# A selective-scan decoder layer: for three of sixteen state indices GpSimd makes u·B in SBUF and ScalarE writes the decay into PSUM

## What is computed

```
xz = x @ W_in.T;  x_ssm, z = split(xz)
x_ssm = silu(causal_conv(x_ssm, 4 taps) + conv_b)
proj = x_ssm @ W_x.T;  B, C = proj[:, 0:16], proj[:, 16:32]
dt = softplus(proj[:, -1:] * W_dt + b_dt);  A = -exp(A_log)
for t in tokens:                       # for every channel d and state n
    h = exp(dt[t] * A) * h + (x_ssm[t] * dt[t]) * B[t]
    y[t] = sum over n of h * C[t]
out = ((y + x_ssm * D) * silu(z)) @ W_out.T
```

## Time and profile before

| | |
|---|---|
| median of 3 runs | 1765.63 us (1763.73 to 1768.42) |
| the profiled execution | 1757.35 us |
| its span in the profile | 1755.6 us |
| granted clock of TensorE, mean | 0.915 of full speed |
| VectorE, TensorE busy | 1421.3 us (81%), 1418.8 us (81%) |
| ScalarE, GpSimd busy | 1151.1 us (66%), 899.1 us (51%) |
| start of the second stage | 1000.2 us |

### The profile page before, as it was taken

One profiled execution on the slowest core, in us unless ns is written; L12 is line 12 of the kernel. 1 busy time (PEld: TensorE's weight loads), 2 busy tenths in 40 slices (PEclk: granted clock), 3 DMA queues, 4 the chain that ended last, 5 costly groups with the idle time before them and its releaser, 6 DMA issues. The chain is left out here.

```text
span 1755.6 us, 23166 instructions
## 1 busy us (share of the span) xinstructions
PE 1418.8 (81%) x7740; PEld 987.4 (56%) x7740; DVE 1421.3 (81%) x2646; ACT 1151.1 (66%) x2516; POOL 899.1 (51%) x659
## 2 busy tenths in 40 slices
PE   7677777877787778778869799888998899888980
PEld 5566665666566656656656445472656355544570
DVE  5999999999999999999999533874667554964578
ACT  5877888788877887788775253377335843476471
POOL 1778777778788878887786000016200630055015
PEclk9799889898989899998989899999999999999895
DMA  7110111011102110121020211000200010000000
GB/s 234 59 55 1 67 67 55 13 67 67 55 13 67 67 62 6 67 67 61 1 85 13 79 34 52 1 1 1 76 1 1 1 45 4 1 1 1 25 1 24
DMA packets 38185, 70.07 MB, mean 40 GB/s; under 512 B 3569, under 2 KB 31826, under 8 KB 33842
## 3 DMA queue, kind: packets, MB, share of 16 engines
q1 hardware_dynamic: 38066, 68.60, 11.5%
HBM read 59.94 MB, written 8.65 MB: 39 GB/s over the span
## 5 line engine op out<-in xcount | busy, mean ns | idle before, releaser
L900 POOL TENSOR_TENSOR state_c<-state,c_area 128x1024 f32<-128x1024 f32 x256 | 600.9, 2357 | 169.4 <-DVE state L970 150.2
L970 DVE TENSOR_TENSOR_SCAN state<-decay,ps 128x512 f32<-128x512 f32 x512 | 620.6, 1212 | 0.0
L686 ACT ACTIVATE decay<-step_area,negA 128x255 f32<-128x255 f32 x1024 | 433.0, 497 | 0.5 <-DVE step_area L1049 0.5
L1577 POOL TENSOR_TENSOR big<-big,g_sb 128x1024 f32<-128x1024 f32 x29 | 78.8, 2718 | 578.9 <-ACT big L1471 577.6
L945 DVE TENSOR_TENSOR ps<-step_area,ps 128x512 f32<-128x512 f32 x512 | 349.9, 684 | 8.3 <-PE ps L368 6.9
L384 PE MATMUL ps<-ident_sb,state_c 128*128 128x128 f32 x2048 | 292.7, 290 | 13.4 <-POOL state_c L900 12.4
L384 PEld LDWEIGHTS ps<-ident_sb,state_c 128*128 128x128 f32 x2048 | 252.4, 150 | 39.8 <-POOL state_c L900 22.4
L368 PE MATMUL ps<-parts,sel_bc_sb 96*128 96x256 bf16 x256 | 74.5, 292 | 104.3 <-DVE ps L961 81.3
L1395 PE MATMUL ps<-w_sb,weights 128*128 128x512 f32 x256 | 129.3, 644 | 0.0
L1430 PE MATMUL ps<-w_sb,hT 128*128 128x256 f32 x512 | 118.9, 386 | 2.5 <-ACT hT L1546 1.9
L1531 ACT ACTIVATE big<-ps 128x1024 f32<-128x1024 f32 x32 | 32.8, 1024 | 121.1 <-PE ps L1395 121.1
(11 more groups left out here) (211 smaller groups left out, 2513.1 us busy)
## 6 DMA issues: line engine op xcount, KB each, us to landing
c_area<-c_scratch SPq DMA_DIRECT2D x32, 1024.0 KB, 6.6
weights<-in_xT SPq DMA_DIRECT2D x16, 256.0 KB, 3.2
res<-in_x SPq DMA_DIRECT2D x16, 256.0 KB, 2.9
x_scratch<-res SPq DMA_DIRECT2D x16, 256.0 KB, 7.9
weights<-x_scratch SPq DMA_DIRECT2D x4, 1024.0 KB, 7.7
xa<-x_scratch SPq DMA_DIRECT2D x4, 1024.0 KB, 5.5
out_x<-acc SPq DMA_DIRECT2D x4, 1024.0 KB, 4.2
w_sb<-in_w SPq DMA_DIRECT2D x2, 1024.0 KB, 12.9
```

Of the source, the lines that this page charges most:

```text
L686: nc.scalar.activation(decay[:, n % RING, j, 1:], dt_sb[:, i[1] % 2, j, 1:], ACT.Exp, scale=negA[:, j * NS + n:j * NS + n + 1]).then_inc(s ...
L900: nc.gpsimd.tensor_tensor(state_c[:, n % RING, :, :], state[:, n % RING, :, :], c_bc[:, q, n, :].unsqueeze(1).to_broadcast([P, CT, TC]), A ...
L970: nc.vector.tensor_tensor_scan(state[:, n % RING, pair, :].rearrange("p j n -> p (j n)"), decay[:, n % RING, pair, :].rearrange("p j n -> ...
L1577: nc.gpsimd.tensor_tensor(tile, tile, g2_sb[:, :], ALU.mult).then_inc(s_gm, 1)
```

## The change

For the states n = 3, 6 and 9 (`OFF`) of every chunk VectorE no longer makes u·B and no longer adds the carry. GpSimd makes the product of 128 x 1024 in SBUF (`product_b`, a ring of two tiles `ub`) from rows of B that a DMA has spread over the partitions (`b_bc`), and adds the carried state into the first column of each tile. ScalarE writes the decays of these states into PSUM (`psum_decay`): the first half into the bank of `b_ps` that is not needed for a row of B, the second into a bank of the three `bu_ps`, with a copy of zeros into the first columns. It does so one state later than before: after its own work for state n+1. The scan of these states reads the decay from PSUM and u·B from SBUF. TensorE issues no `b_row` for them, and `b_row` of state n+2 waits for the first scan of state n.

GpSimd makes the product of state 6 at its place 2, that of state 9 at place 5, and that of state 3 of the next chunk at place 15 (for the first chunk ahead of its first state). SyncE stores 32 rows of B and C instead of 16, and issues one more spreading DMA per chunk, of three rows. To make room in SBUF, w1 and w2 are loaded at the start of the second stage.

```diff
+        OFF, APART = (3, 6, 9), 3
...
+        def bu_free(i, n, h):
+            p = USERS.index((n, h))
+            return scanned(i if p >= 3 else shift(i, -1), *USERS[p - 3])
...
             def load_c(k):
                 q = k[1] % 2
                 sp.wait_ge(s_projc, at(k, 2, 1))
-                sp.dma_start(c_dram[bass.ds(at(k, NS), NS), :], proj[NS:BC, q, :]).then_inc(s_cst, 16)
+                sp.dma_start(bc_dram[bass.ds(at(k, BC), BC), :], proj[0:BC, q, :]).then_inc(s_cst, 16)
                 count = at(k, 16, 16)
                 sp.wait_ge(s_cst, count)
+                if not is_first(k):
+                    sp.wait_ge(s_ub, at(k, 2 * NO))
+                rows = bc_dram[bass.ds(at(k, BC, OFF[0]), APART * NO), :].rearrange("(a s) n -> a s n", s=APART)
+                sp.dma_start(b_bc[:, :, :], rows[:, 0, :].partition_broadcast(P)).then_inc(s_bb, 16)
                 sp.wait_ge(s_y, count)
...
             def b_row(i, n):
+                if n in OFF:
+                    return
                 if n == 0:
                     pe.wait_ge(s_split, at(i, 2, 2))
-                pe.wait_ge(s_bu, at(i, 4 * NS, 4 * n + 4))
+                if n - 2 in OFF:
+                    pe.wait_ge(s_scan, scanned(i, n - 2, 0))
...
             def step(i, n):
-                for j in range(CT):
-                    if j == 0:
-                        if n == 0:
-                            act.wait_ge(s_dt, at(i, 1, 1))
-                        act.wait_ge(s_scan, at(i, 2 * NS, 2 * n + 2))
-                        if n >= RING or not is_first(i):
-                            nc.scalar.activation(carry[:, (n - RING) % NS, :], state[:, n % RING, :, TC - 1],
-                                                 ACT.Copy).then_inc(s_carry, 1)
-                    nc.scalar.activation(decay[:, n % RING, j, 1:], dt_sb[:, i[1] % 2, j, 1:], ACT.Exp,
-                                         scale=negA[:, j * NS + n:j * NS + n + 1]).then_inc(s_decay, 1)
+                act.wait_ge(s_scan, at(i, 2 * NS, 2 * n + 2))
+                if n == 0:
+                    act.wait_ge(s_dt, at(i, 1, 1))
+                if n >= RING or not is_first(i):
+                    nc.scalar.activation(carry[:, (n - RING) % NS, :], state[:, n % RING, :, TC - 1],
+                                         ACT.Copy).then_inc(s_carry, 1)
+                if n in KEPT:
+                    for j in range(CT):
+                        nc.scalar.activation(decay_tile(i, n)[:, j, 1:], dt_sb[:, i[1] % 2, j, 1:], ACT.Exp,
+                                             scale=negA[:, j * NS + n:j * NS + n + 1]).then_inc(s_decay, 1)
+                if n - 1 in OFF:
+                    psum_decay(i, n - 1)
+
+            def psum_decay(i, n):
+
+                for h in range(2):
+                    if h == 0:
+                        act.wait_ge(s_bu, at(i, 4 * NK, 8 + 4 * rank(n - 2) + 3))
+                    else:
+                        act.wait_ge(s_scan, bu_free(i, n, 1))
+                    bank = (b_ps[n % 2] if h == 0 else bu_bank(i, n, 1))[:, :].rearrange("p (j n) -> p j n", j=2)
+                    nc.scalar.activation(bank[:, :, 0], zeros[:, :], ACT.Copy)
+                    for e in range(2):
+                        j = 2 * h + e
+                        nc.scalar.activation(bank[:, e, 1:], dt_sb[:, i[1] % 2, j, 1:], ACT.Exp,
+                                             scale=negA[:, j * NS + n:j * NS + n + 1]).then_inc(s_decay, 1)
...
+            def product_b(i, n):
+
+                c, later = OFF.index(n), i[1] % CPB
+                if c == 0:
+                    pool.wait_ge(s_u, at(i, 1, 1))
+                    pool.wait_ge(s_bb, at(i, 16, 16))
+                if c >= 2:
+                    pool.wait_ge(s_scan, scanned(i, OFF[c - 2], 1))
+                elif not is_first(i):
+                    pool.wait_ge(s_scan, scanned(shift(i, -1), OFF[c - 2], 1))
+                tile = ub_tile(i, n)
+                nc.gpsimd.tensor_tensor(tile, u_sb[:, i[1] % 2, :, :], b_bc[:, c, :].unsqueeze(1).to_broadcast([P, CT, TC]),
+                                        ALU.mult).then_inc(s_ub, 1 if later else 2)
+                if later:
+                    if c == 0:
+                        pool.wait_ge(s_inj, at(i, 2, 1))
+                    pool.wait_ge(s_ub, at(i, 2 * NO, 2 * c + 1))
+                    nc.gpsimd.tensor_tensor(tile[:, :, 0], tile[:, :, 0], inject[:, n, :], ALU.add).then_inc(s_ub, 1)
...
                 work.append((4, lambda: injections(i, NS - RING, NS)))
+                work += [(2, lambda: product_b(i, OFF[1])), (5, lambda: product_b(i, OFF[2]))]
+                if prepare:
+                    work.append((15, lambda: product_b(k, OFF[0])))
...
+            product_b(first, OFF[0])
             turns(pool, turn)
...
             def make_bu(i, n, h):
 
+                if n in OFF:
+                    return
...
             def scans(i, n, h):
...
+                if n in OFF:
+                    if h == 0:
+                        dve.wait_ge(s_ub, at(i, 2 * NO, 2 * OFF.index(n) + 2))
+                    a = b_ps[n % 2] if h == 0 else bu_bank(i, n, 1)
+                    b = flat(ub_tile(i, n))
+                else:
+                    dve.wait_ge(s_bu, at(i, 4 * NK, 8 + 4 * rank(n) + 2 * h + 2))
+                    a, b = flat(decay_tile(i, n)), bu_bank(i, n, h)[:, :]
+                dve.wait_ge(s_decay, at(i, NS * CT, EMIT.index(n) * CT + 2 * h + 2))
+                nc.vector.tensor_tensor_scan(state[:, n % RING, pair, :].rearrange("p j n -> p (j n)"), a, b,
+                                             0.0, ALU.mult, ALU.add).then_inc(s_scan, 1)
...
+            sp.dma_start(w1_sb[:, :, :], w1).then_inc(s_const, 16)
+            sp.dma_start(w2_sb[:, :, :], w2).then_inc(s_const, 16)
```

More of the change, by code:

```diff
@@ L43, with mamba_block @@
 TG = 4
-def mamba_block(nc, x, xT, w_in, w_x, w_out, par, ident_sb, ident, sel_bc, sel_p, c_dram, x1, ahead, s_ahead, ps, early, late, shared,
+def mamba_block(nc, x, xT, w_in, w_x, w_out, par, ident_sb, ident, sel_bc, sel_p, bc_dram, x1, ahead, s_ahead, ps, early, late, shared,
                 w, ctxT):
@@ L64, in mamba_block @@
         SKIP_AT = 8
+        OFF, APART = (3, 6, 9), 3
+        KEPT = [n for n in range(NS) if n not in OFF]
+        NO, NK = len(OFF), len(KEPT)
+        USERS = [(n, h) for n in range(NS) for h in range(2) if n in KEPT or h == 1]
+        EMIT = []
+        for n in range(NS):
+            if n in KEPT:
+                EMIT.append(n)
+            if n - 1 in OFF:
+                EMIT.append(n - 1)
         w_ssm, diag_w, xi, w_gate, xT_sb, w_x_sb = (early[n] for n in ("w_ssm", "diag_w", "xi", "w_gate", "xT", "w_x"))
@@ L83, in mamba_block @@
         state_c = sb("state_c", [P, RING, CT, TC])
+        ub = sb("ub", [P, 2, CT, TC])
+        b_bc = sb("b_bc", [P, NO, TC])
+        zeros = sb("zeros", [P, 2])
         carry = sb("carry", [P, NS, CT])
@@ L148, in mamba_block @@
         s_bu = sem("s_bu")
+        s_ub = sem("s_ub")
+        s_bb = sem("s_bb")
         s_scan = sem("s_scan")
@@ L186, in shift, with rank, scanned, bu_bank @@
             return (i[0], i[1] + n)
+        def rank(n):
+            return sum(m < n for m in KEPT)
+        def scanned(i, n, h):
+            return at(i, 2 * NS, 2 * RING + 2 * n + h + 1)
+        def bu_bank(i, n, h):
+            return bu_ps[at(i, len(USERS), USERS.index((n, h))) % 3]
+        def bu_free(i, n, h):
+            p = USERS.index((n, h))
+            return scanned(i if p >= 3 else shift(i, -1), *USERS[p - 3])
+        def decay_tile(i, n):
+            return decay[:, at(i, NK, rank(n)) % RING, :, :]
+        def ub_tile(i, n):
+            return ub[:, at(i, NO, OFF.index(n)) % 2, :, :]
         def is_first(i):
@@ L905, in turn @@
                             what()
+            nc.gpsimd.memset(zeros[:, :], 0.0)
             nc.gpsimd.memset(decay[:, :, :, 0], 0.0).then_inc(s_zero, 1)
@@ L941, in make_bu @@
                 if h == 0:
[L942 to L945 removed]
+                    dve.wait_ge(s_b, at(i, NK, rank(n) + 1))
+                dve.wait_ge(s_scan, bu_free(i, n, h))
+                nc.vector.tensor_tensor(bu_bank(i, n, h)[:, :].rearrange("p (j n) -> p j n", j=2),
                                         u_sb[:, i[1] % 2, 2 * h:2 * h + 2, :],
@@ L952, in add_carry @@
                 m = 2 * n + h
-                if i[1] % CPB == 0:
+                if i[1] % CPB == 0 or n in OFF:
                     return
@@ L1063, in _, with attn_ffn_block @@
             round_neg(1)
-def attn_ffn_block(nc, x1, ctxT, ident_sb, w, ps, late, shared, g2, be2, bias_rows, before, out):
+def attn_ffn_block(nc, x1, ctxT, ident_sb, w, w1, w2, ps, late, shared, g2, be2, bias_rows, before, out):
     U = G * NL
@@ L1081, in sem @@
             return ctx.enter_context(nc.semaphore(name))
-        wq_sb, wk_sb, wv_sb, wo_sb, w1_sb, w2_sb = (w[n] for n in ("wq", "wk", "wv", "wo", "w1", "w2"))
```

(9 more changed lines are left out.)

27 lines of the change are left out of this document (12 added, 15 removed).

## The result

The changed kernel takes 1823.8 us (median of 4 runs, 1823.22 to 1832.23), the kernel before beside it 1764.68: a ratio of 1.0355, 95% interval [1.0303, 1.0408]. It is slower, by 59 us where I had said 46 (1812 against 1765.63), inside the range. Single executions of one kernel scatter: those of the kernel before lie between 1750 and 1769 us, so a few microseconds of a total say little, and the traces are needed for the parts.

A forecast was written before the change was run, and what follows sets the result against it. A ring between GpSimd and ScalarE, as long as VectorE's chunk, was taken to bound it: 13 x (62.0 - 58.0) = +52, first chunks -4, total +48, 1757.35 to 1805; 8.3 median offset gives 1814, stated 1812, range 1795 to 1828.

The forecast's parts named there:

- The ring: Per-chunk loop softplus, make_dt, GpSimd's work to the mean, spreads, ScalarE's work to softplus: 58.2 us becoming 62.0; chance 0.72.
- GpSimd's part: Ring from make_dt to the mean's end, 20.08 us: state 3's product at place 15 adds 2.6 us.
- ScalarE's part: Ring from spreads to softplus's end: 38.24 us becomes 39.5, +1.2 us.
- the second take_xi is at 5.35 ... the first take_conv is at 9.8: ScalarE's times after spreads: second take_xi at 5.35 us instead of 4.05, first take_conv at 9.8.
- the walk: Step-by-step timing of ScalarE from spreads: second take_conv at 15.2 instead of 15.32, then +1.4 us to softplus.
- +1.3 for the decays of state 3: ScalarE behind spreads: state 3's decays make the second take_xi 1.3 us later, taken back at the second take_conv.
- Rival 3: More than the ring: TensorE's lower clock doubles a 3.5 us conv, or b_bc lands late; +2 us per chunk, 1838; chance 0.10.
- the 0.4 us: ScalarE's 12 activations into PSUM, 0.03 us faster each: 0.4 us a chunk, not counted, left in the range.
- idles 8 us a chunk: Sign: VectorE idles some 8 us per chunk, mostly before state 3's scan, ended by ScalarE's exponential into PSUM.
- The first two chunks: No centre there, so they follow VectorE; could give 7.4 us, half taken: -4.
- The last chunk: Late centre and psum_decay(3) cost VectorE about 4.5 us against 3.8 saved; attention starts later: 0 to +3, taken as 0.
- The second stage: Moved loads of w1 and w2 (2 MB) behind its other loads: nothing, or 0 to 5 us once.

The follow-up runs named there:

- e7: Kernel before plus nine small unread GpSimd products at place 15, between make_dt and the mean; ratio 1.0254, period 61.76 us.
- e8: Kernel before plus the same nine small unread GpSimd products at place 6, between the mean and make_dt; ratio 0.9994, period 58.45 us.
- e1: Changed kernel with GpSimd's product of state 3 moved from place 15 to place 0, behind the mean; ratio to the kernel before 1.0144, period 59.69 us.
- e12: Changed kernel with GpSimd's three products cut from 256 to 16 time steps; ratio to the kernel before 1.0187, period 60.34 us.
- e2: Changed kernel with ScalarE's PSUM decay of state 3 made ahead of spreads; ratio to the kernel before 1.0408, period 62.83 us.
- e14: Changed kernel moving only states 6 and 9, products at places 2 and 6, with e10's later places; ratio to the kernel before 1.0002, period 58.09 us.
- e10: Kernel before with spreads, guess, normalise at places 6, 10, 13 and variance, newton at 5, 9; ratio 0.9957, period 58.07 us.
- e3: Changed kernel with spreads, guess, normalise at places 6, 8, 11 and variance, newton at 5, 7; ratio to the kernel before 1.0177, period 60.42 us.
- e15: Changed kernel moving only states 6 and 9, products at places 2 and 6, other places unchanged; ratio to the kernel before 1.0067, period 59.32 us.
- e9: Changed kernel with state 3's product at place 0, its decays ahead of spreads, and e10's later places; ratio to the kernel before 1.0135, period 59.64 us.
- e13: e9 with GpSimd's three products cut from 256 to 16 time steps; ratio to the kernel before 1.0133, period 59.64 us.

## Why the prediction was right, and where it was off

**The ring** was the mechanism. e7 shows that it had no slack (3.05 us in, 3.7 out), e8 that GpSimd's time outside it is free, e1 and e12 that of three products one counts. That the moved work makes the other work slower by itself is ruled out by the list of groups: GpSimd's product with the row of C takes 2354 ns (before 2357), VectorE's scan 1213 (before 1212).

**GpSimd's part** was right: 20.08 + 2.6 = 22.68, measured 22.71. The product takes 2.37 us (mean 2368 ns), the column add 0.20.

**ScalarE's part** was mis-sized: +1.2 predicted (39.5), 40.67 measured in that chunk and +2.1 over the 13 periods (40.01 against 37.94). The failing step is "the second take_xi is at 5.35 ... the first take_conv is at 9.8". They came at 5.59 and 11.18, and from there the walk held: second take_conv at 16.47 (said 15.2), then 24.20 us to the end of softplus (said 24.3; before 22.92). I had taken TensorE's durations from before. But the longer wait of spreads is also an idle time of TensorE ahead of in_proj, behind which in_proj took 3.78 us and not 1.99, the eight matmuls of L429 behind it took 1.92 and not 1.04, and conv started at 472.79, 7.3 us after spreads and not at the 6.2 that a take_conv at 9.8 implies (4.84 in the kernel before). The term that I put at that place, +1.3 for the decays of state 3, was covered by it (e2). Rival 3 had named this clock, with the right unit (an operation at half pace), and gave it to the conv; it fell on in_proj and on L429, and cost 1.2 us in this chunk and not 2. Over the 13 periods the second take_conv is 0.8 us later than before (15.80 against 15.03) where I had said 0.1 earlier, and what stands behind it grew by 1.3 us where I had said 1.4.

The Trainium skill ("ScalarE: Activation LUTs", the remark on ScE→PSUM under "Step-by-step: what each stage is for") would have made the ring shorter by the faster destination. Here a single exponential of 128x255 lasts 459 ns into PSUM and 496 into SBUF, which agrees with it, but a row of four into SBUF takes 1.69 us and one of two into PSUM 0.86, both at a pace of 0.40 us: in a row nothing is won at this width, and to leave the 0.4 us out was right.

**VectorE** idles 8 us a chunk, as said, but not most of it before the scan of state 3. Of 102 us from 165 to 960 us, 37 lie before the first scan of state 3, 28 before the product of state 11, 21 before the next chunk's first product and 13 before that of state 5, whose rows TensorE delivers late. (Before state 3 the waits view names GpSimd eight times. The product of GpSimd that the scan needs, four states back, had ended long before, and ScalarE's second exponential ended 0.13 us before the scan each time.) Its timeline:

```profile
465.93 1.21 DVE L1065 TENSOR_TENSOR_SCAN state<-decay,ps 128x512 f32<-128x512 f32 x1
469.92 1.22 DVE L1065 TENSOR_TENSOR_SCAN state<-ps,ub 128x512 f32<-128x512 f32 x1 [2.78 <-ACT ps L747]
...
476.82 0.70 DVE L1032 TENSOR_TENSOR ps<-step_area,ps 128x512 f32<-128x512 f32 x1 [1.82 <-PE ps L413]
```

The scan that reads its decay from PSUM has the same duration as the other (1210 and 1213 ns in the list of groups). The new load of b_bc is never what a product waits for:

```profile
L952 POOL TENSOR_TENSOR ub<-step_area,b_bc 128x1024 f32<-128x1024 f32 x48 | 113.7, 2368 | 27.5 <-DVE step_area L1146 27.5
```

**The first two chunks** gave 0.7 us and not 4. The first distance between two make_dts is 56.9 us where it was 57.0. I had let them follow VectorE. e14 and e10 suggest that they follow the passage between ScalarE and TensorE, which the change does not shorten; no run took those chunks alone. In e3, which differs from the changed kernel only from the third chunk on, the same distance is 58.3, so one such distance is good to a microsecond or two.

**The last chunk** cost 12.5 us where I had said 0 to +3. This is the largest single miss. My step "VectorE loses about 4.5 us against the 3.8 it saves" left out that `b_row` of state 7 stands behind the attention's first matmuls in TensorE's order, and that there is no row of state 6 between them any more, with which VectorE was kept busy. Behind a wait for ScalarE four of 128x512 took 3.75 us, where the same four take 1.96 in the kernel before (at 917.87), and VectorE's product waited 10.51 us, where the longest wait there is 1.80. Part of the 12.5 may be scatter: the same stretch takes 118.9 us in e8, 4 us more than in the kernel before, though no work was added to its last chunk. TensorE's timeline, then VectorE's:

```profile
983.07 3.75 PE L482 MATMUL ps<-wv_sb,ctx_sb 128*128 128x512 f32 x4 [1.95 <-ACT weights L754]
986.75 2.07 PE L483 MATMUL ps<-bv_sb,ones 1*128 1x512 f32 x2
...
994.81 0.28 PE L413 MATMUL ps<-parts,sel_bc_sb 96*128 96x256 bf16 x1
```

```profile
995.13 0.70 DVE L1032 TENSOR_TENSOR ps<-step_area,ps 128x512 f32<-128x512 f32 x1 [10.51 <-PE ps L413]
```

**The second stage** was 5.6 us shorter where I had said 0 to +5 for the moved loads of w1 and w2. The loads are not the reason. In e10, which does not move them, the stage takes 749.64 us, in e12 and e15, which do, 756.24 and 756.43. The length goes with the clock that TensorE was granted in that stage: 0.930 in the changed kernel and in e10, 0.923 in the kernel before, 0.922 in e12 and e15. At the same clock the moved loads make a difference of 0.15 us (749.79 against 749.64). What sets the clock of that stage in an execution stays open.

The slips against each other: 13 x (4.6 - 4.0) = +8, first chunks +3, last chunk +12.5, second stage -5.6, which is the 18 us between the +48 of the sum and the 66.0 of the two spans. The forecast missed by only 12, and that was luck: 1812 stands 7 us above the sum's 1805, because the profiled execution of the kernel before lies 8.3 us under its median, and that of the changed kernel lies only 0.4 under its own (1823.42 against 1823.8). The number was in the range because the range held a ring of 63.2.

**What stays open** is the last 1.55 us a chunk of e9 against e14. The products are excluded (e13). That leaves the decays of state 3 with their 2.7 us of waiting for banks, and TensorE's clock (0.87 against 0.88 in e14), and no run parts them. Other places for that one state were not tried.

## What to carry to other kernels

Before work is moved to the engine with time to spare, follow each pair of engines that wait for each other once per round and add up the ring they make: here work put inside it cost its full length and more, the same work outside it nothing that could be measured (e7, e8), and a share of busy time shows neither. Do not count the ring's own waits for a third engine as slack. Then ask what else is as long as the engine that is to be relieved; two of the three moved states, placed well, left the period where it was although VectorE had 30 us less to do. If TensorE will idle longer than before, as it did here with 5.5 us instead of 2.2, reckon with the work behind it at the lower clock's pace.

## What the runs showed of the hardware

After 5.47 us without work TensorE took 3.78 us for eight matmuls of 128x256 that take 1.99 us after 1.97 us without work, and the next eight of L429 1.92 instead of 1.04: a ratio near 2, as between its two levels of 1.2 and 2.4 GHz. The granted clock of the chunk fell from 0.91 to 0.83 with it, and over all 13 periods from 0.91 to 0.86. e7 shows the same (3.51 us after 5.74) without any other part of the change. The idle time just before does not decide it alone: the kernel before has the slow pace too, in three of 13 chunks, once after 1.64 us without work, and the fast one after 2.89. So a wait of one engine was paid a second time by another: 3.0 us more in GpSimd's part came with 0.7 more in ScalarE's (e7), and GpSimd's 2.6 us came back as 3.0 us a chunk when it was taken out (e1).
